# Head of chunk 1 in the recurrent layer: TensorE's three products one step later, the affine step on ScalarE, the product with delta on GpSimd, border decays ahead of the gate

## The reference, cut to what matters

```python
xn = layernorm(x, ln1_g, ln1_b)
delta = softplus(xn @ Wd.T + bd)
bc = xn @ Wbc.T + bbc                      # Bm, Cm: 16 states each
# for every position t, 16 states per feature:
#   h = exp(delta_t * A) * h + delta_t * B_t * xn_t ;  y = sum_n h * C_t
ssm_out = x + y + D * xn
```

## Time and profile before

| | us |
|---|---|
| median of 3 runs | 1958.9 (1958.1 to 1959.21) |
| the profiled execution | 1957.49 |
| its span, first to last instruction | 1955.8 |
| TensorE busy | 1495.6 (76%) |
| VectorE busy | 1460.2 (75%) |
| ScalarE busy | 1133.2 (58%) |
| GpSimd busy | 885.1 (45%) |
| mean granted TensorE clock | 0.896 of full |

### The profile page before, as it was taken

How to read it: one execution, slowest core, us unless ns; L and a number is a source line. 1 busy time by engine, 2 the same in 40 slices (tenths; PEclk the granted TensorE clock), 3 DMA queues, 4 the chain that set the end, 5 groups by cost and what they waited for, 6 DMA issues and landing times.

```text
span 1955.8 us, 16370 instructions
## 1 busy us (share of the span) xinstructions
PE 1495.6 (76%) x5225; PEld 643.0 (33%) x5296; DVE 1460.2 (75%) x1790; ACT 1133.2 (58%) x1539; POOL 885.1 (45%) x578
## 2 busy tenths in 40 slices
PE   5899896788877786788887768678887674654766
PEld 2444342334433232334333323233443221111222
DVE  2582386999487878689767769589948778998953
ACT  3447564776527476568626667468553655445555
POOL 2041252555018772455206775254502873573455
PEclk9999997999989798899989889789998986686989
DMA  7000000001101000000100010000100200000000
GB/s 182 1 33 22 1 12 0 22 1 37 39 1 33 22 22 1 1 22 1 65 11 3 30 42 2 0 22 1 65 11 0 97 22 22 1 0 1 0 11 11
DMA packets 12599, 42.42 MB, mean 22 GB/s; under 512 B 1866, under 2 KB 1890, under 8 KB 10466
## 3 DMA queue, kind: packets, MB, share of 16 engines
q1 hardware_dynamic: 11698, 35.08, 4.9%
q0 software_dynamic: 816, 6.30, 1.5%
HBM read 38.23 MB, written 4.19 MB: 22 GB/s over the span
## 4 chain that ended last, share of the span: by engine, by line
DVE 35%; PE 27%; issue 17%; ACT 10%; POOL 9%; another core or an unknown queue 2%; DMA 0%; POOLq 0%; SPq 0%; DVEq 0%; ACTq 0%
DVE st L2196 7%; PE psf L1456 4%; DVE psu L2181 4%; PE psu L1641 3%; DVE sy L2210 3%; PE psf L1346 2%; PE psy L1626 2%; POOL ap L751 2%; POOL gate L746 2%; DVE g1p L1974 2%; POOL gx L728 2%; PE psy L1718 2%; DVE low L2006 1%; DVE lin L2322 1%
## 5 line engine op out<-in xcount | busy, mean ns | idle before, releaser
L728 POOL TENSOR_TENSOR gx<-gx,sy 128x1024 f32<-128x1024 f32 x120 | 295.4, 2462 | 240.2 <-DVE sy L2210 239.2
L746 POOL TENSOR_TENSOR gate<-gate,lin 128x512 f32<-128x512 f32 x120 | 155.0, 1291 | 408.6 <-DVE lin L2329 402.2
L2181 DVE TENSOR_TENSOR psu<-so,psu 128x1024 f32<-128x1024 f32 x128 | 156.5, 1222 | 70.3 <-remote 48.6
L719 POOL TENSOR_TENSOR g2p<-tf,g2p 128x512 fp32r<-128x512 f32 x64 | 86.6, 1354 | 264.7 <-ACT g2p L928 264.7
L1102 ACT ACTIVATE gate<-gate 128x512 f32<-128x512 f32 x128 | 80.3, 628 | 206.6 <-DVE gate L2318 206.4
L1456 PE MATMUL psf<-g1p,h2w 128*128 128x512 f16 x768 | 187.5, 394 | 2.0 <-DVE sy L2210 1.4
L1018 ACT ACTIVATE da<-delta,aneg 128x512 f32<-128x512 f32 x256 | 163.4, 710 | 7.0 <-DVE st L2196 6.4
L2210 DVE TENSOR_TENSOR sy<-st,psu 128x1024 f32<-128x1024 f32 x128 | 156.0, 1219 | 9.5 <-DVE st L2196 5.2
L2196 DVE TENSOR_TENSOR_SCAN st<-da,carry,psu 128x512 f32<-128x512 f32 x128 | 156.8, 1267 | 6.8 <-ACT carry L1024 5.0
L1742 PE MATMUL psu<-ap,mw 128*128 128x512 f16 x384 | 108.8, 413 | 64.2 <-POOL ap L751 64.2
L2196 DVE TENSOR_TENSOR_SCAN st<-da,psu 128x512 f32<-128x512 f32 x128 | 149.0, 1205 | 1.5
(11 more groups left out here) (391 smaller groups left out, 3361.7 us busy)
## 6 DMA issues: line engine op xcount, KB each, us to landing
mw<-in_mlp_w SPq DMA_DIRECT2D x3, 2048.0 KB, 8.1
xn<-in_x SPq DMA_DIRECT2D x8, 512.0 KB, 6.5
wf<-in_wf SPq DMA_DIRECT2D x4, 1024.0 KB, 4.8
xr<-in_x SPq DMA_DIRECT2D x8, 512.0 KB, 3.9
x<-gx SPq DMA_DIRECT2D x8, 512.0 KB, 3.8
out<-outc SPq DMA_DIRECT2D x8, 512.0 KB, 3.1
mw<-in_mlp_w SPq DMA_DIRECT2D x3, 1024.0 KB, 10.2
h1w<-in_h POOLq DMA_DIRECT2D x1, 2048.0 KB, 12.7
```

The source lines that it names most:

```text
L719: pool.tensor_tensor(g2p[:, m % 2, 1], tf[:, m % 2], g2p[:, m % 2, 0].bitcast(F32), ALU.subtract).then_inc(g2_lo.sem, 1)
L728: pool.tensor_tensor(out, chunk(gx, c), sy[:, n % 2], ALU.add).then_inc(y_acc.sem, 1)
L746: pool.tensor_tensor(gate[:, r % NG], gate[:, r % NG], lin_at(b, r)[:], ALU.mult)\
L2181: dve.tensor_tensor(input_banks(n), chunk(so, c), both(psu[:, row_bank(n)]), ALU.mult)\
```

## The change

On TensorE the head products of chunk 1 in a batch stand in steps 9, 10 and 11. The affine step is done by ScalarE in all eight heads, by two activations (Identity with scale and bias) that wait for `head_norm` and give the signal `head_norm1` gave. The product of delta and xn for chunk 1 (four heads) is made by GpSimd after its add of step 13 in a batch, of step 10 in the closing; it waits for the D*xn instruction. For chunk 0 it stays on VectorE. In a batch ScalarE does decays 18 and 19 at the end of step (0, 15) and no longer at the end of step (1, 0).

```diff
 # GpSimd
+            def head_product(b):
+
+                pool.wait_ge(le_step.sem, le_step.at(b, NC * LE_STEPS))
+                pool.tensor_tensor(chunk(so, 1), delta[1][:], xn1(b, 1), ALU.mult).then_inc(head_done.sem, 1)
 # batch, after state_add(b1, c, n)
+                        if (c, n) == (0, 13):
+                            head_product(b1)
 # closing, after state_add(b, 0, n)
+                    if n == 10:
+                        head_product(b)
 # ScalarE
+            def head_affine(b, c):
+                act.wait_ge(le_step.sem, le_step.at(b, LE_STEPS * c + 2))
+                for t in range(KD):
+                    last = act.activation(xn1(b, c)[:, t], xn1(b, c)[:, t], ACT.Identity, scale=col("ln1_g", t),
+                                          bias=col("ln1_b", t))
+                last.then_inc(le_step.sem, 1)
 # opening, chunk 1
-                                                 (12, softplus, 0), (13, head_b16, 0)):
+                                                 (10, head_affine, 0), (12, softplus, 0), (13, head_b16, 0)):
 # batch, chunk 0
-                            for at, piece in ((SQUARE_AT, head_square), (B16_SIDE_AT, head_b16), (PLUS_AT, softplus)):
+                            for at, piece in ((SQUARE_AT, head_square), (8, head_affine), (B16_SIDE_AT, head_b16),
+                                              (PLUS_AT, softplus)):
-                        if c == 1 and n == 0:
+                        if c == 0 and n == NS - 1:
                             decay(b1, NS + 2)
                             decay(b1, NS + 3)
 # expert stage
-                            for at, piece in ((14, head_square), (16, head_root), (23, softplus),
+                            for at, piece in ((14, head_square), (16, head_root), (19, head_affine), (23, softplus),
 # closing
-                    for at, piece, c in ((1, head_square, 1), (1, expert_root, 0), (3, head_root, 1), (5, head_b16, 1),
+                    for at, piece, c in ((1, head_square, 1), (1, expert_root, 0), (3, head_root, 1), (5, head_affine, 1), (5, head_b16, 1),
 # TensorE, batch
-                            for at, piece in ((4, head_mean), (6, head_var), (8, head_delta0), (9, head_delta1),
-                                              (10, head_bc)):
+                            for at, piece in ((4, head_mean), (6, head_var), (9, head_delta0), (10, head_delta1),
+                                              (11, head_bc)):
 # VectorE
-            def head_norm1(b, c):
-                for t in range(KD):
-                    last = dve.tensor_scalar(xn1(b, c)[:, t], xn1(b, c)[:, t], col("ln1_g", t), col("ln1_b", t),
-                                             ALU.mult, ALU.add)
-                head_step(b, c, HEAD_STEPS, last)
 # head_late
-                head_step(b, c, LE_STEPS, last)
-
-                dve.tensor_tensor(chunk(so, c), delta[c][:], xn1(b, c), ALU.mult).then_inc(head_done.sem, 1)
+                if c == 0:
+                    head_step(b, c, LE_STEPS, last)
+                    dve.tensor_tensor(chunk(so, c), delta[c][:], xn1(b, c), ALU.mult).then_inc(head_done.sem, 1)
+                else:
+                    last.then_inc(le_step.sem, 1)
```

More of the change, by code:

```diff
@@ L2359, in opening @@
                     for at, piece, b in ((5, l0_center, 1), (6, head_center, 0), (8, l0_scale, 1), (9, head_norm, 0),
-                                         (9, head_norm1, 0), (10, head_z0, 0), (11, head_z1, 0), (12, head_parts, 0),
+                                         (10, head_z0, 0), (11, head_z1, 0), (12, head_parts, 0),
                                          (12, head_softplus, 0), (13, head_late, 0)):
@@ L2399, in batch @@
                         if b1 is not None and c == 0:
-                            for at, piece in ((4, head_center), (7, head_norm), (8, head_norm1), (9, head_z0),
+                            for at, piece in ((4, head_center), (7, head_norm), (9, head_z0),
                                               (10, head_z1), (11, head_parts), (12, head_softplus),
@@ L2434, in batch @@
                                     piece(b0, c, wave)
-                            for at, piece in ((14, head_center), (18, head_norm), (19, head_norm1), (20, head_z0),
+                            for at, piece in ((14, head_center), (18, head_norm), (20, head_z0),
                                               (22, head_z1), (24, head_parts), (26, head_softplus),
@@ L2486, in closing @@
                 head_norm(b, 1)
-                head_norm1(b, 1)
                 state_input(b, 0, 5)
```

## The result

| | before | after |
|---|---|---|
| median of the runs | 1958.97 us (1958.10 to 1959.21, 4 runs) | 1898.39 us (1893.97 to 1902.85, 4 runs) |
| profiled execution, span | 1957.5, 1955.8 us | 1902.69, 1901.0 us |
| steps 8 to 13 of chunk 0, batch 2 | 66.98 us | 45.95 us |

The ratio is 0.9692, with a 95% interval of 0.966 to 0.9723: 60.6 us less. The forecast was 1890. The changed kernel's own runs lie 9 us apart, two near 1894 and two near 1903, where those of the kernel before lie 1 us apart. In the later runs the kernel before lay up to 5 us apart as well (1956.92 to 1961.96), so a difference of a few us between two kernels is not shown by the totals alone.

What follows compares the result with a forecast made beforehand. No engine's total decides; in chunk 0's scan VectorE and TensorE wait for each other. Gains 65.1 + 1.6 + 2.0 + 0 = 68.7 us from 1957.5 give 1888.8, plus 1.4 for the median: 1890; range 1883 to 1900.

Steps and rivals of the forecast that it cites:

- The mechanism: Chunk 0's scan beside chunk 1's head: products one step later end TensorE and VectorE's mutual waits; 65.1 us in three batches.
- Step 8: Step 8 of chunk 0's scan, affine gone from VectorE: 4.76 + 1.3 = 6.1 us, before 14.09.
- The other rule it weighed: VectorE up to about 3 times ScalarE's rate: moving the affine would lose 1.0 us in each of eight heads, sum 1898.
- Steps 9 to 13: Chunk 0's scan: step 9 takes 6.6 us, step 11 8.5 (half clock 1.3 more), steps 12 and 13 together 16.1.
- Rival A: Clock stays low: sixteen-matmul tasks take twice as long in steps 9 to 11, about 10 us a batch; 1920 us, chance 0.14.
- B (more): VectorE becomes the only bound, expert-stage and closing bounds hold: 1875 us; chance 0.12 for something between 1885 and 1875.
- The affine on ScalarE: Affine pair beside the stall takes ScalarE 1.50 us: cost 0, at most 1.5 us a batch.
- The product on GpSimd: Chunk 1's product behind VectorE's last head step in step 13: cost 0, bounds 0 and 2.5 us a batch.
- Border decays: Decays 18 and 19 before the gate: gate about 2.2 us later, fourth silu relieved; 0, bounds -2.1 and +3.8 a batch.
- Rival C: Stall only changes place, head gains nothing, gate late behind the decays loses 3.8 us a batch: 1966 us, chance 0.04.
- Expert stage: Three chunk 0 heads: affine ends some 0.5 us earlier on ScalarE, 1.6 us gained; bounds 1.94 and -1.5 each.
- Closing: Affine's 1.66 us become a wait, gain 0; product with delta leaves VectorE, gain 2.0 us; bounds 0 and 3.7.

Runs made afterwards that it cites:

- Experiments 1 and 2: First: kernel before with only TensorE's head products one step later, 1912.81 us. Second: changed kernel with those products back in steps 8, 9 and 10, 1937.28 us.
- experiment 10: Kernel before, with GpSimd's add of step 8 of chunk 0 also waiting for VectorE's input of step 9: 1953.41 us.
- Experiment 4: Changed kernel, with GpSimd's state add of step 8 of chunk 0 also waiting for VectorE's input of step 9, batches only: 1883.62 us.
- kernel 5: Changed kernel, with GpSimd's state adds of steps 4 to 8 in both chunks waiting for VectorE's input of the next step, batches only: 1861.02 us.
- experiment 3: Changed kernel with decays 18 and 19 back in the first step of chunk 1: 1894.93 us.
- Experiment 6: Changed kernel with the affine pair of chunk 0's three heads in the expert stage back on VectorE: 1894.61 us.
- experiment 8: Changed kernel with the product with delta of chunk 1 (four heads) back on VectorE: 1901.55 us.
- Experiment 7: Changed kernel with 24 one-column memsets on VectorE behind the output of step 14 of chunk 1 in the first batch, results unused: 1894.26 us.

## Why the prediction was right, and where not

**The mechanism was right.** Experiments 1 and 2 show it from both sides: the table line alone takes steps 9 and 10 from 13.3 and 13.9 to 6.5 and 6.8 us, and taking it back brings 12.2 and 15.0. Forecast 68.7 us on the profiled execution, measured 54.8 there and 60.6 between the medians. The time, 1898.39, lies inside the stated range of 1883 to 1900, but near its edge. Of the 13.9 us that the profiled execution lacks, 3.0 are missing in the head's steps; 11.6 were lost in step (1,10) and in the late stretches, against small gains elsewhere.

**Step 8 is the term that was mis-sized.** "VectorE: 4.76 + 1.3 = 6.1" came out as 8.1. The 1.3 was the pair g1p as it stood behind the affine. In the place directly behind the output it starts together with GpSimd's state add and takes 3.46. The affine's 3.04 was read as its price, though it was 1.00 of work [experiment 10] and 2 of waiting for that add; taking the affine away handed the wait to the next instruction. Experiment 4 gives the forecast 6.0 once the add is out of the way. The Trainium skill's "SBUF — State Buffer", who interferes with whom, has the rule: a VectorE instruction with two SBUF inputs and a GpSimd one that reads SBUF block each other. The rows of g1p at 3.46 and 1.29 agree: the first g1p of the pair (0.68 us) held up the add by 0.4, and the add held up the second by 2.2. The prediction asked this of the instructions behind the moved product in steps 14 and 15, and did not ask it of the one that moved up in step 8. Its reading there holds (the inputs still take 1.22). The other rule it weighed, the Trainium skill's VectorE for mul and add ("ScalarE: Activation LUTs", rules for kernel authors), holds for the bare operation: 1.00 us on VectorE alone against 1.51 on ScalarE. The Trainium skill gives its "up to about 3×" there for bf16, and the prediction's loss of 1.0 us a head took it over for an fp32 pair, where the rows show 1.5. What decided was the add beside it, and that ScalarE had the time.

**Steps 9 to 13 came out as worked out**: 6.6, 6.8, 8.5, 7.8 and 8.2 us, for 6.6, 6.5, 8.5 and 16.1 together. The clock held: granted 1.00 over the stretch. The prediction took the middle of 23.2 (full clock) and 20.1 (half); with the full clock and the 2.1 missing in step 8, 23.2 - 2.1 = 21.1, and batches 2 and 3 gave 21.0 and 21.1. Three batches: 62.1 against 65.1. So two errors met in this term: the clock was better than the middle and step 8 worse, and that the term came out only 3 us off is in part luck. Rival A (a clock that stays low) is out by the 1.88 rows, and B (more) too, although kernel 5 shows that 1861 was to be had.

**The affine on ScalarE costs nothing** where it stood beside the stall, as forecast. It runs ahead of the input of step 8 and ends 4.3 us before product 0 starts. ScalarE, scan of chunk 0 in the changed kernel:

```profile
740.86 1.51 ACT L1005 ACTIVATE so<-so,pk 128x512 f32<-128x512 f32 x2
```

**The product on GpSimd** was put at 0 in the scan, and is. The 1.14 it frees are in step 13's 8.2 us. GpSimd's row in the changed kernel:

```profile
787.66 2.39 POOL L733 TENSOR_TENSOR so<-delta,so 128x1024 f32<-128x1024 f32 x1 [0.63 <-DVE gx L2183]
```

It starts 0.1 us behind VectorE's last head step. "Its readers come two steps later" was wrong for one of them: ScalarE's decays for the first steps of chunk 1 are issued in step 14 already and wait for it, changed kernel, ScalarE:

```profile
790.08 2.56 ACT L1034 ACTIVATE da<-delta,aneg 128x512 f32<-128x512 f32 x4 [0.81 <-POOL so L733]
```

The wait is 0.81 us and VectorE's steps 14 and 15 (4.8 and 5.7 us) are no longer for it than before the change.

**Border decays: loss and gain cancel**, the parts as named; the gate came 2.1 us later for 2.2 forecast. Step (1,0) grew by 3.4 us, (1,1) and (1,2) fell by 2.3 and 1.3, and experiment 3 finds 26.1 for 25.9. Rival C took the border at its upper bound, a loss of 3.8 a batch; step (1,0) alone lost 3.4, but the two steps behind it gave it back, and the head's gain, which C had at nothing, came.

**Expert stage, opening, closing.** Expert stage: forecast 0.5 a head. Changed kernel, first batch, TensorE and VectorE:

```profile
623.77 3.78 PE L1571 MATMUL psf<-xn,wd 128*128 128x512 f32 x4 [1.73 <-ACT xn L1005]
```
```profile
627.60 0.75 DVE L2154 TENSOR_SCALAR zt<-psf,pk 128x512 f32<-128x512 f32 x1 [3.06 <-PE psf L1571]
```

In this head TensorE's wait fell from 2.37 to 1.73. In the other two it reads 4.06 and 4.09, because TensorE was done earlier with what stands in front; so the time from the norm's second instruction on VectorE to the first z is the better measure: 8.48 us for 9.11 between their starts in all three, 0.6 less. VectorE's wait for z rose by 1.35 of the 1.94 that the affine had taken. Experiment 6 can't see it in the total. Opening: 0, the first batch starts at 236.8 and 236.9. Closing: 2.1 for the product, by steps and by experiment 8 (forecast 2.0), and nothing for the affine, whose 1.66 us turned into a wait as named: steps (0,4) and (0,5) of the last batch are 7.9 + 10.4 for 9.6 + 8.8 (18.3 for 18.4).

**What was not foreseen is the loss elsewhere**: 4.8 us in step (1,10) and 6.8 in the late stretches. The first is a step of 5.2, 6.4 or 7.6 us in the two traces of the changed kernel, and where it is longer the input waits for TensorE. Changed kernel, batch 1, VectorE:

```profile
435.74 1.23 DVE L2194 TENSOR_TENSOR psu<-so,psu 128x1024 f32<-128x1024 f32 x1 [1.42 <-PE psu L1597]
```

Its window in the changed kernel, and that of the same step in the kernel before (columns as in the windows above):

```profile
429.35:435.74 6.39, 6.17 (x24) 2.88 (x24) 4.90 (x6) 2.53 (x5) 4.80 (x3) 0.81 0.00 0
```
```profile
449.60:454.79 5.19, 5.05 (x23) 2.54 (x24) 4.89 (x5) 2.42 (x5) 4.76 (x3) 1.00 0.00 0
```

In all thirteen traces this step stands three times. The 22 that take 5.2 us have a granted clock of 1.00, the 17 longer ones one of 0.76 to 0.92. So this loss goes with a lower granted clock: the sixteen-matmul task in it takes 4.46 us in the changed kernel's batch 1, and 3.62 in its second trace, where the step takes 5.2. Why the clock falls in one execution and not in another isn't shown.

The second shows in the windows from the last state input of batch 3 to the first of batch 4, changed kernel and kernel 3:

```profile
1339.40:1564.80 225.40, 171.58 (x535) 72.69 (x540) 158.52 (x255) 116.73 (x157) 99.45 (x75) 0.90 0.11 42
```
```profile
1335.50:1557.50 222.00, 169.37 (x535) 71.74 (x540) 157.62 (x256) 115.88 (x156) 100.44 (x75) 0.92 0.11 43
```

The same 535 matmul records take 2.2 us more of TensorE and the stretch 3.4 us more, at a granted clock of 0.90 for 0.92. The kernel before had 221.3 there, kernel 8 had 221.0. Here the longer time goes with a lower granted clock. But it doesn't everywhere: in the first batch the stretch took 227.7 us at 0.92 in the changed kernel and 226.9 at 0.90 in the kernel before. The three stretches together took 675.3 us before, 682.1 and 679.1 in the two traces of the changed kernel, and 674.7 and 674.0 in kernels 3 and 8, which keep every edit in these stretches. So it is no price of the edits there, and its cause stays open. Nor do whole runs decide it: in the first four runs of the changed kernel the two near 1903 have a mean clock of 0.905 and 0.904, the two near 1894 one of 0.908, but kernel 6 has 1894 to 1895 at 0.902 to 0.909. Experiment 7 was to move the stages in time, and didn't by enough to tell.

## What to carry to other kernels

Write down, for two engines that hand work back and forth in fixed orders, which instruction of which step each waits for: a result at the end of one engine's step that the other needs within the same step makes the two work in turn, and one line of an order table can be worth more than work taken off the busiest engine (46 us here, against 21 for all the other edits). Before you take an instruction's traced duration as what its removal gives, look at what another engine does in the same microseconds: a wait hidden in a duration does not leave with the instruction, but goes to the next one of its kind. Then look whether the other side of that collision has slack, and let it wait (37 us here for a condition and a wait, 31 of them in the steps named there), but not where its own queue is followed by work that a later step needs.

## What the runs showed of the hardware

A pair of VectorE instructions with two SBUF inputs and fp16 output (128x512) took 1.29 us alone and 3.46 beside a GpSimd fp32 add of 128x1024, and the add 2.35 to 2.41 alone and 2.75 beside it; of the pair, the instruction that started before the add took 0.68 and the one behind it 2.86. An fp32 pair with one SBUF tensor input and two per-partition operands took 1.00 alone and 3.04 beside the add. State inputs and outputs, with an operand in PSUM, took 1.22 us in the mean of all their 128 rows (1.21 to 1.23), with an add beside them or not. And one program's eight runs lay 9 us apart (1893.97 to 1902.85): one of its steps took 5.2 us at a granted clock of 1.00 and 6.4 or 7.6 at 0.81 or 0.77, with the same instructions.
